# Two stages of a decoder kernel: x and the context brought in already turned, instead of turned by PE

## The reference, cut to what matters

```python
cq  = x @ Wc + bc          # 512 -> 128
ckv = x @ Wckv + bckv      # 512 -> 128
q   = cq @ Wcq + bcq;  qr = cq @ Wqr + bqr
k   = ckv @ Wck + bck; kr = x @ Wkr + bkr; v = ckv @ Wv + bv
...
k2  = ctx @ Wk + bk        # 512 -> 4 heads of 128
v2  = ctx @ Wv + bv
```

## Time and profile before

| what | value |
|---|---|
| median of 3 runs | 3014.51 us (3012.94 to 3017.65) |
| the profiled execution | 3019.52 us, its span 3017.7 us |
| PE busy | 2734.9 us (91%) |
| DVE busy | 2017.4 us (67%) |
| ACT busy | 1669.3 us (55%) |
| POOL busy | 1790.0 us (59%) |
| mean granted TensorE clock | 0.949 of full speed |
| chain that ended last | PE 49%, POOL 23%, DVE 14%, issue 7%, ACT 4%, DMA 3% |
| first stage | 0 to about 112 us |
| second stage | about 112 to 665 us |

### The profile page before, as it was taken

How to read it: one execution, slowest core, us unless ns; L and a number is a source line. 1 busy time by engine, 2 the same in 40 slices (tenths; PEclk the granted TensorE clock), 3 DMA queues, 4 the chain that set the end, 5 groups by cost and what they waited for, 6 DMA issues and landing times.

```text
span 3017.7 us, 47826 instructions
## 1 busy us (share of the span) xinstructions
PE 2734.9 (91%) x15794; PEld 2442.4 (81%) x15794; DVE 2017.4 (67%) x3921; ACT 1669.3 (55%) x4244; POOL 1790.0 (59%) x2193
## 2 busy tenths in 40 slices
PE   8699999978999999997699789999999996979998
PEld 7588887857888888875599678888888885869998
DVE  5477777755887888887356456767667676864334
ACT  2265555536888888774455455555655552643222
POOL 0277777734676777665246287888898896630000
PEclk9799999987999999998799899999999998989999
DMA  6635554544433333332411321212212202532101
GB/s 213 197 113 169 155 158 150 155 152 137 129 96 113 114 103 109 108 92 84 140 51 52 127 82 64 93 44 66 78 58 64 74 30 78 178 122 77 33 28 33
DMA packets 209286, 310.76 MB, mean 103 GB/s; under 512 B 47351, under 2 KB 104739, under 8 KB 206931
## 3 DMA queue, kind: packets, MB, share of 16 engines
q1 hardware_dynamic: 209042, 307.70, 32.6%
HBM read 211.27 MB, written 96.37 MB: 102 GB/s over the span
## 4 chain that ended last, share of the span: by engine, by line
PE 49%; POOL 23%; DVE 14%; issue 7%; ACT 4%; DMA 3%; SPq 0%; POOLq 0%; ACTq 0%; DVEq 0%
PE bank L168 9%; PE bank L169 8%; PE bank L170 8%; POOL mh_quant_d L747 6%; PE bank L1621 4%; POOL mh_quant_d L741 3%; POOL mh_quant_d L743 3%; POOL mh_quant_d L745 3%; PE bank L1605 3%; PE bank L1562 3%; POOL me_rl L3171 2%; PE bank L1026 1%; PE bank L1595 1%; PE bank L2091 1%; PE bank L2092 1%
## 5 line engine op out<-in xcount | busy, mean ns | idle before, releaser
L747 POOL TENSOR_TENSOR mh_quant_d<-mh_quant_a,mh_quant_d 128x512 f32<-128x512 f32 x208 | 283.2, 1361 | 17.3
L822 ACT ACTIVATE mh_quant_d<-mh_quant_d 128x512 f32<-128x512 f32 x256 | 161.5, 631 | 229.0 <-POOL mh_quant_d L747 228.6
L725 DVE TENSOR_REDUCE mh_quant_err<-mh_quant_d 128x8 f32<-128x512 f32 x256 | 173.6, 679 | 56.5 <-ACT mh_quant_d L822 54.4
L741 POOL TENSOR_SCALAR mh_quant_d<-mh_quant_a 128x512 f32<-128x512 f32 x208 | 142.0, 683 | 87.2 <-DVE mh_quant_err L725 48.5
L2321 POOL TENSOR_TENSOR fq_var<-fq_mv,eps_ln 100x1 f32<-100x1 f32 x16 | 3.7, 230 | 315.4 <-DVE fq_mv L2264 315.4
L1605 PE MATMUL bank<-ga_eT,ga_v 128*128 128x400 f32 (+1 forms) x384 | 170.9, 527 | 10.6 <-DVE ga_zl L1792 10.6
L1562 PE MATMUL bank<-ga_xt,ga_wqh 128*128 128x400 f32 x512 | 178.4, 411 | 1.6 <-DVE ga_xt L164 1.6
L1756 ACT ACTIVATE ga_e<-ga_e,ga_nm 100x361 f32<-100x361 f32 x256 | 152.7, 596 | 42.5 <-DVE ga_nm L1851 40.4
L780 POOL TENSOR_TENSOR ga_quant_d<-ga_quant_a,ga_quant_near 128x512 f32<-128x512 f32 x128 | 165.3, 1292 | 13.4 <-DVE ga_quant_err L725 2.9
L1752 ACT ACTIVATE ga_e<-ga_e,ga_rs 100x361 f32<-100x361 f32 x256 | 152.5, 596 | 19.2 <-DVE ga_rs L1833 19.2
L1879 POOL TENSOR_TENSOR ga_qrs<-ga_qms,minus_half 100x4 f32<-100x4 f32 x64 | 68.2, 1065 | 158.9 <-DVE ga_qms L1786 158.9
(11 more groups left out here) (435 smaller groups left out, 10356.1 us busy)
## 6 DMA issues: line engine op xcount, KB each, us to landing
keys_turned<-kv_kt SPq DMA_DIRECT2D x16, 1448.0 KB, 6.0
ga_kt<-keys_turned SPq DMA_DIRECT2D x64, 362.0 KB, 3.0
ga_xt<-x_turned SPq DMA_DIRECT2D x48, 400.0 KB, 5.0
mh_xt<-x_turned SPq DMA_DIRECT2D x48, 400.0 KB, 4.7
kv_rows<-qkv SPq DMA_DIRECT2D x50, 320.0 KB, 3.4
qkv<-m_rows SPq DMA_DIRECT2D x16, 960.0 KB
raw<-x SPq DMA_DIRECT2D x64, 200.0 KB
kv_ctx<-in_ctx SPq DMA_DIRECT2D x32, 256.0 KB, 4.7
```

Of the source, the lines that this page charges most:

```text
L725: nc.vector.tensor_reduce(self.of(self.err, i)[:, s, :], self.error(i, s), AX, ALU.add).then_inc(self.summed.sem, 1)
L741: nc.gpsimd.tensor_scalar(e, a[:], 1.0 / SHRINKS[s], MAGIC, ALU.mult, ALU.add).then_inc(made.sem, 1)
L747: nc.gpsimd.tensor_tensor(e, a[:], e, ALU.subtract).then_inc(self.diff.sem, 1)
L822: nc.scalar.activation(self.error(i, s), self.error(i, s), ACT.Square).then_inc(self.squared.sem, 1)
```

## The change

The program gets two more inputs, made ahead of its start from x and the context: `x_turned`, with 128 features on the first axis, then the 4 blocks of features, then all 1600 tokens; and `ctx_turned`, per batch with 128 features, 4 blocks and 361 keys. The old inputs stay, since x is also added as rows.

First stage: x is loaded as [128, 4, 400] per group in four loads, one per block of features (128 pieces of 1600 bytes), into two tiles. The 64 transposes, their semaphore and the two banks fall away. ACT and DVE split per block of features instead of per batch, from SBUF instead of a bank. Products of block k in the first of the two results wait only for that block. SP issues the four loads of the second group ahead of the small loads; the third group's wait for the remainders of the first, and the fourth group's for those of the second.

Second stage: the context part is loaded as [128, 4, keys] (512 pieces of 512 or 420 bytes, instead of 128 or 105 of 2 KB). The 192 transposes fall away, `ctx_hi` waits for the load, and `ctx_hi` and `ctx_lo` read SBUF instead of a bank. SP's next load waits for `ctx_lo`. `turn_attended` has its bank for itself and no longer waits for `ctx_lo`.

```diff
-        x = [sb(f"{ph}_x{n}", [S, D], F32, ctx) for n in range(XR)]
+        x = [sb(f"{ph}_x{n}", [P, KC, N], F32, ctx) for n in range(2)]
...
-        def turned_after(b_):
+        def parted_after(b_):
...
             def load_x(e):
-                sp.dma_start(x[e % XR][:], rows_of(x0, e)).then_inc(x_in[e % XR].sem, 16)
+                g, k = divmod(e, KC)
+                sp.dma_start(x[g % 2][:, k, :], t["x_turned"][:, k, g * N:(g + 1) * N]).then_inc(x_in[e % (2 * KC)].sem, 16)
...
             for n in range(1, NW):
                 load_weight(n)
+            for e in range(4, 8):
+                load_x(e)
             small_load()
...
-            for e in range(XR, 2 * XR):
-                since(sp, x_turned, e - XR)
+            for e in range(8, 12):
+                since(sp, x_lo, e - 8)
                 load_x(e)
             for b_ in range(B):
-                for e in turned_after(b_):
-                    if e + XR < B:
-                        sp.wait_ge(x_turned.sem, x_turned.upto(e))
-                        load_x(e + XR)
+                for e in parted_after(b_):
+                    if e >= 4 and e + 8 < KC * BG:
+                        sp.wait_ge(x_lo.sem, x_lo.upto(e))
+                        load_x(e + 8)
...
         def do_pe():
-            def turn_x(e):
-                pe.wait_ge(x_in[e % XR].sem, x_in[e % XR].upto(e // XR))
-                since(pe, x_lo, e - 2)
-                for k in range(KC):
-                    last = nc.tensor.transpose(x_bank[e % 2][:, k * S:(k + 1) * S], x[e % XR][:, k * P:(k + 1) * P], ident[0:S, 0:S])
-                last.then_inc(x_turned.sem, 1)
-
             def features(g):
-                since(pe, x_lo, G * g + G - 1)
...
                     for k in range(KC):
+                        if n == 0:
+                            since(pe, x_lo, KC * g + k)
...
-            def turned_hi(e):
-                g, j = divmod(e, G)
-                act.wait_ge(x_turned.sem, x_turned.upto(e))
-                if j == 0:
+            def x_part_hi(e):
+                g, k = divmod(e, KC)
+                since(act, x_in[e % (2 * KC)], g // 2)
+                if k == 0:
                     since(act, out_full, NO * (G * (g - 1)) - 1)
-                copy_hi(xh[g % 2][:, :, cols(j)], x_bank[e % 2][:, 0:KC * S].rearrange("p (k s) -> p k s", k=KC)).then_inc(x_hi.sem, 1)
+                copy_hi(xh[g % 2][:, k, :], x[g % 2][:, k, :]).then_inc(x_hi.sem, 1)
...
-                sub_lo(xl[g % 2][:, :, cols(j)], x_bank[e % 2][:, 0:KC * S].rearrange("p (k s) -> p k s", k=KC),
-                       xh[g % 2][:, :, cols(j)]).then_inc(x_lo.sem, 1)
+                sub_lo(xl[g % 2][:, k, :], x[g % 2][:, k, :], xh[g % 2][:, k, :]).then_inc(x_lo.sem, 1)
...
-        cin = [sb(f"{ph}_ctx{n}", [P, D], F32, ctx) for n in range(4)]
+        cin = [sb(f"{ph}_ctx{n}", [P, KC, P], F32, ctx) for n in range(4)]
...
-                sp.dma_start(cin[s % 4][0:KEYS[n], :], ctxv[j, n * P:n * P + KEYS[n], :]).then_inc(ctx_in[s % 4].sem, 16)
+                sp.dma_start(cin[s % 4][:, :, 0:KEYS[n]], t["ctx_turned"][j, :, :, n * P:n * P + KEYS[n]]).then_inc(ctx_in[s % 4].sem, 16)
...
                 if 0 <= c and c + 4 < NS:
-                    sp.wait_ge(turned_c.sem, turned_c.upto(c))
+                    sp.wait_ge(c_lo.sem, c_lo.upto(c))
                     load_ctx(c + 4)
...
-            def turn_ctx(s):
-                kk = rows(s)
-                pe.wait_ge(ctx_in[s % 4].sem, ctx_in[s % 4].upto(s // 4))
-                since(pe, c_lo, s - 1)
-                for k in range(KC):
-                    last = nc.tensor.transpose(ctx_bank[:, k * P:k * P + kk], cin[s % 4][0:kk, k * P:(k + 1) * P],
-                                               ident[0:kk, 0:kk])
-                last.then_inc(turned_c.sem, 1)
...
-                since(pe, c_lo, min(NS - 1, last_quad[b_] + 5 - SH))
...
-                if 0 <= c + 1 < NS:
-                    turn_ctx(c + 1)
...
-                act.wait_ge(turned_c.sem, turned_c.upto(s))
+                since(act, ctx_in[s % 4], s // 4)
                 since(act, v_full, s - 2)
-                copy_hi(ch[s % 2][:, :, 0:kk], ctx_bank[:].rearrange("p (k c) -> p k c", k=KC)[:, :, 0:kk])\
-                    .then_inc(c_hi.sem, 1)
+                copy_hi(ch[s % 2][:, :, 0:kk], cin[s % 4][:, :, 0:kk]).then_inc(c_hi.sem, 1)
...
-                sub_lo(cl[s % 2][:, :, 0:kk], ctx_bank[:].rearrange("p (k c) -> p k c", k=KC)[:, :, 0:kk],
-                       ch[s % 2][:, :, 0:kk]).then_inc(c_lo.sem, 1)
+                sub_lo(cl[s % 2][:, :, 0:kk], cin[s % 4][:, :, 0:kk], ch[s % 2][:, :, 0:kk]).then_inc(c_lo.sem, 1)
...
+    feeds["x_turned"] = feeds["x"].reshape(T, KC, P).transpose(2, 1, 0)
+    feeds["ctx_turned"] = feeds["ctx_2048"].reshape(B, S2, KC, P).transpose(0, 3, 2, 1)
```

More of the change, by code:

```diff
@@ L367, in mla_project @@
         ph, ctx, G = "m1", ExitStack(), 4
-        N, BG, XR, RR = G * S, B // G, 4, 4
+        N, BG, RR = G * S, B // G, 4
         quarter = lambda n: raw[n // 4][:, n % 4 * 512:(n % 4 + 1) * 512]
@@ L397, in mla_project @@
         rows = [sb(f"{ph}_rows{n}", [S, H, ROW], F32, ctx) for n in range(RR)]
-        x_bank, c_bank, out_bank = bank[0:2], bank[2:4], bank[4:8]
+        c_bank, out_bank = bank[2:4], bank[4:8]
         NO = len(out_bank)
@@ L403, in mla_project @@
         brr_in = Signal(f"{ph}_brr_in", 1, 32)
-        x_in = [Signal(f"{ph}_x_in{n}", B // XR, 16) for n in range(XR)]
+        x_in = [Signal(f"{ph}_x_in{n}", BG // 2, 16) for n in range(2 * KC)]
         rows_out = [Signal(f"{ph}_rows_out{n}", B // RR, 32) for n in range(RR)]
-        x_turned, x_hi, x_lo = (Signal(f"{ph}_{c}", B) for c in ("x_turned", "x_hi", "x_lo"))
+        x_hi, x_lo = (Signal(f"{ph}_{c}", KC * BG) for c in ("x_hi", "x_lo"))
         c_full, c_hi, c_lo = (Signal(f"{ph}_{c}", 2 * BG) for c in ("c_full", "c_hi", "c_lo"))
@@ L509, in project @@
                 out(3, 1, wkv, 512, 512).then_inc(out_full.sem, 1)
-            for e in range(G):
-                turn_x(e)
             features(0)
@@ L539, in do_act @@
             weight_hi(0)
-            for e in range(G):
-                turned_hi(e)
+            for e in range(KC):
+                x_part_hi(e)
             for n in range(1, NW):
@@ L583, in do_dve @@
             weight_lo(0)
-            for e in range(G):
-                turned_lo(e)
+            for e in range(KC):
+                x_part_lo(e)
             for n in range(1, NW):
@@ L606, in mla_project @@
                [(s_.sem, s_.upto(s_.events - 1)) for s_ in rows_out])
-        for s_ in (w_in + x_in + rows_out + [w_hi, w_lo, brr_in, x_turned, x_hi, x_lo, c_full, c_hi, c_lo, out_full, biased, padded]):
+        for s_ in (w_in + x_in + rows_out + [w_hi, w_lo, brr_in, x_hi, x_lo, c_full, c_hi, c_lo, out_full, biased, padded]):
             s_.hand_back()
@@ L883, in kv_and_attend @@
         qz = Quantiser(ph, ctx, t["L1_ffn_w_fc"], w_fc_q, 0, NC, on_pool=True, depth=2, on_dve=QUANT_ON_DVE)
-        ctx_bank, kt_bank, k_bank, v_bank, qk_bank, score_bank, turn_bank, out_bank = bank
+        a_bank, kt_bank, k_bank, v_bank, qk_bank, score_bank, turn_bank, out_bank = bank
         ctx_in = [Signal(f"{ph}_ctx_in{n}", NS // 4, 16) for n in range(4)]
@@ L892, in kv_and_attend @@
         one = lambda name: Signal(f"{ph}_{name}", NS)
-        turned_c, k_full, v_full, k_turned = one("ctx_turned"), one("k_full"), one("v_full"), one("k_turned")
+        k_full, v_full, k_turned = one("k_full"), one("v_full"), one("k_turned")
         c_hi, c_lo, k_sq, k_hi, v_made = one("ctx_hi"), one("ctx_lo"), one("k_squared"), one("k_hi"), one("v_made")
@@ L1046, in turn_attended @@
                 pe.wait_ge(at_in.sem, at_in.upto(b_))
-                since(pe, c_lo, min(NS - 1, last_quad[b_] + 5 - SH))
                 for k in range(KC):
-                    last = nc.tensor.transpose(ctx_bank[:, k * S:(k + 1) * S], at[:, k * P:(k + 1) * P], ident[0:S, 0:S])
+                    last = nc.tensor.transpose(a_bank[:, k * S:(k + 1) * S], at[:, k * P:(k + 1) * P], ident[0:S, 0:S])
                 last.then_inc(turned_a.sem, 1)
```

11 lines of the change are left out of this document (5 added, 6 removed).

## The result

| | before | after |
|---|---|---|
| median | 3014.86 us (3012.01 to 3018.38, 10 runs) | 3006.67 us (3000.39 to 3012.72, 10 runs) |
| ratio after / before | | 0.9972, 95% interval 0.9962 to 0.9982 |
| the profiled execution | 3019.52 us, span 3017.7 | 3008.59 us, span 3006.8 |
| first score of the second stage starts at | 118.42 us | 115.74 us |
| from first to last score (50 steps) | 515.86 us | 514.79 us |

The kernel is 8.2 us faster, 5.4 to 11.5 by the interval. 3005.2 was forecast, in a range from 2997 to 3014: both held. The last row of the table can't be credited to the change: the code behind the last score is the same, and eleven traced executions of kernels that share it have 2376.2 to 2383.9 there. That none of it comes from the change isn't shown.

The account below looks back on a forecast made before the run. PE was taken to bound 24.5 to 99 us, its waits the start, and PE with DVE and POOL the second stage. Terms -1.6 - 11.1 + 3.4 = -9.3 us gave 3010.2 profiled, 3005.2 median, range 2997 to 3014.

Parts of the forecast that it names:

- Small loads at 20.3, clock falls: +2.5 us: Start: small loads land at 20.3 behind 819 KB of x, costing 1.0 us, and PE's clock falls, costing 1.5.
- the first rival: Start: small loads not delayed or PE stays warm, start gives about -2.5 instead of +2.5, 3000 us; chance 0.17.
- The clock in the start: Start: PE idle 4.5 us after its first 24 products, clock falls to 1.2 GHz, slow stretch costs 1.5 us.
- Six pairs of turns, -4.1 us: First stage after the start: twelve transposes in six pairs left out, each 0.69 us on the chain, -4.1 us.
- First stage: -1.6 forecast: Whole first stage: -4.1 us from the turns and +2.5 us at the start, -1.6 us.
- 25 turns give all, one gives half: -10.3 us: Second stage: 25 transpose groups on the chain give 9.9 us, one at the slow clock gives 0.4.
- Five of the nine others give nothing, four give 0.19: Second stage, steps after an output projection: key projection also waits for DVE's kv_x addition; nine turns give 0.8 us.
- DVE's reads, +3.4 us: Second stage: ctx_lo from two SBUF tiles takes 0.21 us more, 48 times, counting in about 16 steps: +3.4 us.
- Rival 3: Second stage: POOL holds ctx_lo in nearly every step; slower, 3021.5 us at 0.65 us hold, 3031 at 0.85; chance 0.07.
- What is late next is POOL's kv_x: Second stage: POOL's kv_x is late next; DVE already waits 17.9 us for it in nine steps; no term.
- rival 2: Second stage: DVE and POOL bind in most steps, some 2 of the net 7.7 us come through, 3011; chance 0.17.
- The context's small pieces, ACT's copies: Second stage: context loads in 512 or 420 byte pieces and ACT's copy from SBUF cost nothing.

Follow-up runs that it names:

- the bias move: POOL's addition of the bias to x put ahead of its wait for the squares' sums: changed kernel 2994.56 us, kernel before 3007.67 us.
- POOL free: Six weight chunks copied unquantised, without POOL's and DVE's quantising beside the second stage: changed kernel 2977.17 us, kernel before 3001.87 us, one execution each.
- kept turns: Changed kernel with PE again doing 4 transposes per context step, for nobody, and SP's next load waiting for them: 3013.23 us, ratio 0.9992.

## Why the prediction was right, and where it was not

The forecast of 3005.2 lies 1.5 us from the median, in its range, with the right sign. That it is so close is luck: two errors cancel. The first stage was said to give 1.6 us and gives 5.4; the second was said to give 7.7 and gives 3.6 (512.3 us from first to last score as the mean of four traces, 515.8 of three with the old one). What it had right is the bound of each stretch, the ties, and what would be late next.

- **Small loads at 20.3, clock falls: +2.5 us. This step failed.** The pads start at 18.75, 17.87, 18.70, 18.13, 17.69 and 18.12 in the six traces with this order, 0.7 us later on average than in five of the old kernel (17.27, 17.70, 17.60, 17.54, 17.51). I added 819 KB at the old rate of 267 GB/s. But the queue was not full at that rate: now it moves 312 GB/s from 6 to 18 us, against 267, which is 12 x 45 = 540 KB more in the same time. I had named this as the evidence for the first rival and given it 0.17. The 0.7 is not what the 819 KB cost, though. In the two traces with the small loads first they land at 16.34 and 15.74, so the 819 KB delay them by 2.2 us, not far from my 3.07. The rest is that the new loads of x and the weights ahead of the small loads are through 1.5 us sooner than the old ones. No run separates what makes them so (their form, 128 pieces on 128 partitions instead of 100 on 100, is a guess).
- **The clock in the start.** It fell behind the idle time in one of the six traces, for PE was idle there for 0.8 to 2.4 us and not 4.5. The 24 products before it were taken at the 5.8 us of the one trace; in thirteen traces they take 5.7 to 7.1 from the first start to the last, with 8 to 17 of their distances at 0.33 us and the others near 0.18. The traces' records of the granted clock begin only about where the distances shorten (at 17.17 us in the kernel before, 16.43 in the changed one), which fits a clock at its lower level until then; the 1.00 that the windows give ahead of that is not measured. DVE's first addition of a bias in the first stage starts at 20.7 on average (21.8, 20.3, 21.1, 20.5, 20.1, 20.5), at 21.7 before (21.2, 21.9, 22.2, 22.4, 20.6): the start gives 0.9 us instead of costing 2.5.
- **Six pairs of turns, -4.1 us: right.** From that first addition (of the bias `bcq`) to the last of the same bias it takes 75.4 us in the five traces of the old stage, 70.7 to 70.8 in five of the new one and 71.5 in the profiled one with the slow start: -4.6. Where the 0.5 us above the six pairs come from is open.
- **First stage: -1.6 forecast.** The first score starts at 118.06 to 119.62 in five traces of the old stage (mean 119.05) and at 112.89 to 115.74 in six of the new one with its order of loads (mean 113.63): -5.4. The profiled execution of the changed kernel was the worst of the six.
- **25 turns give all, one gives half: -10.3 us: right in sum.** The 35 steps gave 9.7 to 10.8 in the four traces without the bias move. It is 28 steps with some 11 us, less the fall of the clock behind 2.13 us of idle PE in the fifth step, for which there was no term.
- **Five of the nine others give nothing, four give 0.19: the tie was read rightly, its cost was not.** With POOL free the 14 steps give 0.20 each, so the earlier trace rows did show where PE's gain ends: PE's output projection, DVE's addition and PE's key projection form a loop that holds only a tail of the turns. But I took these steps as they stood. With POOL's rounds packed closer, the key projection started 0.3 to 0.4 us later on average, +4.1 to +5.1 in all.
- **DVE's reads, +3.4 us: size off.** The mean of kv_cl is 0.76 to 0.78 us against a forecast of 0.85 to 0.95 (0.645 before), and the kept turns price the whole at +2.0, of which 1.2 is PE's own. Rival 3, a mean above 1.2, is out. That POOL is lengthened in turn had no term of its own.
- **"What is late next is POOL's kv_x": named, and costed at nothing. This is the second step that failed.** It is the mechanism of rival 2 at the steps with an output projection, though not in most steps. There it costs the +4 to +5 us (some 1.2 of it also with the turns kept) and, where PE idles for over 2 us, up to three falls of the clock of 1.5 us, for which the sum had no term in this stage. The earlier trace rows had both ends of it, an idle time of 1.50 us without a fall and one of 3.80 with it.
- **The context's small pieces, ACT's copies: nothing, right.** The context part lands in 4.8 us at the median (4.7 before), and no wait for it stands among the waits.
- The section Who interferes with whom of the page SBUF — State Buffer in the Trainium skill has the right pair of instructions: kv_cl is lengthened when POOL quantises and not otherwise. Its hold for a whole instruction could have cost up to one of POOL's operations a piece, 1.29 us for the longest common one; the mean rose by 0.13 us (0.645 to 0.779; the longest took 1.45), and the trace decides.

The best kernel of these runs that differ by more than noise is the changed one with POOL's bias early, 20.4 us below the kernel before, of which the change itself gives 13.1; with the small loads first as well it is the same within noise.

## What to carry to other kernels

Before an engine is made faster, mark the steps in which another engine's result arrives within a few tenths of it, and follow that result back: what stands ahead of it in its engine's stream is what the gain will meet. An operation whose inputs are ready long before (here a bias on x) should not stand behind a wait in that stream. And one profiled execution shows one draw of the clock: repeat it before a difference of a few microseconds is explained.

## What the runs showed of the hardware

- Granted TensorE clock: idle times of PE between 2.0 and 2.8 us were followed by the lower level in some executions and not in others, at the same place in the same code. Behind 2.79 to 2.82 us it fell in two of four traces of the changed second stage, behind 2.32 or 2.33 in two, and behind 2.01 to 2.03 in two. In three of these six falls the products had gone on at the higher level for 1.0 to 1.5 us first. Behind 2.13 to 2.16 us at another place it fell in all six. At the start it fell after 2.16 us (changed kernel). It stayed up after 2.40 us (start, first stage alone), 2.07 (kept turns) and 1.93 to 1.95. The length of the idle time alone didn't decide in this range.
- A queue that moved 267 GB/s over 12 us, busy for 0.78 of them, had room: it moved 312 with 819 KB more in the same stretch. Loads behind those 819 KB landed at 17.7 to 18.8 us with them ahead and at 15.7 and 16.3 without: 2.2 us on average, where the old rate gave 3.1.
- A DVE subtraction with both inputs in SBUF: 691 ns for 128x512 without POOL's quantising, 758 with it, and for 128x420 596 and 823. POOL's quantiser operations beside it took 5.6% longer in all (253.5 to 267.8 us).
